# Sums of squares in column tiles, state products ahead of the last third of the output products, and drained blocks ahead of the weights' low part, in a Mamba-2 mixer on one core

## What is computed

```
proj = xn @ in_proj_w.T                       # gate 8192, hs 8192, B 1024, C 1024, dt 128
hBC  = silu(conv4(proj part) + conv_b)        # causal convolution of 4 taps
X    = hs * dt                                # 128 heads of 64 channels, chunks of 128 tokens
Y_diag = ((C B^T) * L) X                      # inside a chunk
states = (B * decay)^T X ; Y_off = C @ running states * exp(A_cs)
xg   = (Y_diag + Y_off + D*hs) * silu(gate)
xr   = xg * rsqrt(mean(xg*xg over a group of 1024 channels) + 1e-5)   # 8 groups
out  = (xr * norm_weight) @ out_proj_w.T      # 8192 -> 512
```

## Time and profile before

| | us |
|---|---|
| median of 3 runs | 1606.25 (1604.5 to 1606.3) |
| the profiled execution, its own time | 1604.1 |
| its span from the first to the last instruction | 1602.4 |
| PE busy in it | 1578.8 (99%) |
| DVE, ACT, POOL busy | 1423.1, 1370.4, 1279.1 |
| granted PE clock | 1.000 |

### The profile page before, as it was taken

One profiled execution on the slowest core, in us unless ns is written; L12 is line 12 of the kernel. 1 busy time (PEld: TensorE's weight loads), 2 busy tenths in 40 slices (PEclk: granted clock), 3 DMA queues, 4 the chain that ended last, 5 costly groups with the idle time before them and its releaser, 6 DMA issues. The chain is left out here.

```text
span 1602.4 us, 29224 instructions
## 1 busy us (share of the span) xinstructions
PE 1578.8 (99%) x9172; PEld 1296.0 (81%) x9172; DVE 1423.1 (89%) x2328; ACT 1370.4 (86%) x2620; POOL 1279.1 (80%) x1614
## 2 busy tenths in 40 slices
PE   9999999999999999999999999999999999999998
PEld 7877888888888888887778788888888888888886
DVE  7989899999999998999979888888888898888887
ACT  4688899999999898988846899989999999899895
POOL 5549998989898998989874487877777777778786
PEclk9999999999999999999999999999999999999999
DMA  5266767677767676676614666766766677667662
GB/s 175 93 186 205 227 188 218 201 209 214 195 218 206 201 224 199 206 206 198 196 40 145 204 208 200 225 202 202 227 189 218 207 204 222 199 205 227 190 218 89
DMA packets 231754, 311.83 MB, mean 195 GB/s; under 512 B 144176, under 2 KB 160560, under 8 KB 231344
## 3 DMA queue, kind: packets, MB, share of 16 engines
q1 hardware_dynamic: 231600, 309.97, 63.9%
HBM read 240.69 MB, written 36.70 MB: 173 GB/s over the span
## 5 line engine op out<-in xcount | busy, mean ns | idle before, releaser
L409 ACT ACTIVATE mt<-cs_row,cs_tok 128x128 f32<-128x128 f32 x1024 | 324.9, 391 | 0.0
L633 POOL TENSOR_TENSOR wl<-raw,wh 128x256 fp32r<-128x256 f32 x328 | 254.4, 807 | 59.3 <-ACT wh L381 59.3
L727 POOL COPY xt<-turned 128x512 uint16<-128x512 uint16 x248 | 206.3, 878 | 58.6 <-DMA turned<-tg 58.2
L718 POOL TENSOR_TENSOR mt<-mt,gt 128x256 f32<-128x256 f32 x128 | 117.8, 942 | 134.3 <-ACT mt L590 134.3
L743 POOL TENSOR_TENSOR sqa<-sqa,sq 128x256 f32<-128x256 f32 x222 | 221.6, 1018 | 0.8 <-ACT sq L563 0.8
L750 POOL TENSOR_TENSOR wol<-raw_o,woh 128x256 fp32r<-128x256 f32 x256 | 183.3, 737 | 39.0 <-ACT woh L530 38.9
L736 POOL TENSOR_TENSOR xl<-xg,xh 128x256 fp32r<-128x256 f32 x254 | 192.2, 778 | 5.1 <-ACT xh L543 5.1
L1093 DVE SCALAR_TENSOR_TENSOR cv<-bt,par_sb,cv 128x511 f32<-128x511 f32 (+2 forms) x192 | 143.8, 749 | 42.5 <-ACT cv L385 37.9
L1093 DVE SCALAR_TENSOR_TENSOR cv<-bh,par_sb,cv 128x511 f32<-128x511 f32 (+2 forms) x192 | 143.7, 748 | 30.8 <-ACT cv L385 25.8
L1323 DVE TENSOR_TENSOR mt<-mt,gt 128x1024 f32<-128x1024 f32 (+1 forms) x128 | 159.7, 1247 | 0.9 <-ACT mt L590 0.9
L381 ACT ACTIVATE wh<-raw 128x1024 fp32r<-128x1024 f32 (+1 forms) x146 | 151.9, 1040 | 0.8 <-DMA raw<-in_w_dtag 0.8
(11 more groups left out here) (217 smaller groups left out, 3819.2 us busy)
## 6 DMA issues: line engine op xcount, KB each, us to landing
raw<-in_w_step SPq DMA_DIRECT2D x128, 512.0 KB, 4.5
cs_row<-cs_rows SPq DMA_DIRECT2D x128, 512.0 KB, 7.0
low_parts<-wl SPq DMA_DIRECT2D x64, 512.0 KB, 5.8
raw_o<-in_w_out SPq DMA_DIRECT2D x128, 256.0 KB, 5.7
wl<-low_parts SPq DMA_DIRECT2D x64, 512.0 KB, 4.7
ec_row<-ec_rows SPq DMA_DIRECT2D x256, 96.0 KB, 5.7
raw<-in_w_bc SPq DMA_DIRECT2D x16, 512.0 KB, 3.5
acc<-in_x SPq DMA_DIRECT2D x8, 256.0 KB, 5.0
```

The source lines that it names most:

```text
L409: e = act.activation(mt[:, m % 2, h, chunk(j)], cs_row[:, m % 2, h, chunk(j)], ACT.Relu, bias=cs_tok[:, j, 2 * m + h:2 * m + h + 1], scale ...
L633: e = pool.tensor_tensor(wl[:, n % 2, cols], raw[:, n % 2, cols], wh[:, n % 2, cols].bitcast(F32), ALU.subtract)
L727: e = pool.tensor_copy(to[:, half], turned[:, NJ * half:NJ * (half + 1), :])
```

## The change

It does five things:

1. `sum_squares` makes the ones (128 by 32) the stationary operand and moves the squares, 128 columns for each of four column tiles of 32. The sums of 32 tokens lie along the free axis, copied to 32 rows of a tile. `mean_square` scales 128 by 128 values into rows and transposes them in blocks of 32 by 32, so that the four columns wanted stand at every 32nd place; both live in `part[:, 0]`, and two waits are added for that (`p_acc` of the group before, `p_lo`).
2. In steps 2 to 63 `output` issues two thirds, then the state products follow, then the last third, then the diagonal products.
3. The wait for `xt` is moved from the state products to the diagonal products (where the tokens were turned by DMA; steps 0 and 63 keep it).
4. In b = 1 `add_drained` adds all three blocks in one step, ahead of `wol`.
5. The dead branches for `TURN_FROM` go, with `pick` and its reduction.

```diff
-        ones = sb("ones", [P, 1])
+        ones = sb("ones", [P, SQ])
+        ms_rows, ms_cols = part[:, 0, P:2 * P], part[:, 0, 0:P]
+        ms = part[:, 0, 0:P:SQ]
...
+                    if b + 1 == NB and has(m - 2) and m > 2 and (m - 2) % PER_GROUP == 0:
+                        add_drained(b, (n - 2) // PER_GROUP - 1, range(ACT_BLOCKS))
                     if has(m - 1):
                         pool.wait_ge(a_woh, did(n - 1))
...
-                    if has(m - 2) and m > 2 and (m - 2) % PER_GROUP == 0:
+                    if b + 1 < NB and has(m - 2) and m > 2 and (m - 2) % PER_GROUP == 0:
                         add_drained(b, (n - 2) // PER_GROUP - 1, range(ACT_BLOCKS - 1))
-                    if has(m - 2) and m > 3 and (m - 3) % PER_GROUP == 0:
+                    if b + 1 < NB and has(m - 2) and m > 3 and (m - 3) % PER_GROUP == 0:
                         add_drained(b, (n - 3) // PER_GROUP - 1, (ACT_BLOCKS - 1,))
...
+                    early_state = has(m) and has(m - 2) and by_dma(b, m - 1)
+                    def sum_squares(dst, src, start=True, stop=True):
+                        of = src[:, :].rearrange("p (j a c) -> p a j c", j=NJ, c=SQ)
                         for a in range(P // SQ):
+                            mm = pe.matmul(dst[SQ * a:SQ * (a + 1), 0:P].rearrange("p (j c) -> p j c", j=NJ), ones[:, :],
+                                           of[:, a], start=start, stop=stop)
+                        return mm
-                        for j in range(NJ):
-                            mm = pe.matmul(dst[:, j:j + 1], sqa[:, chunk(j)], ones[:, 0:1],
-                                           start=True, stop=True)
...
                         if has(m - 2):
-                            output()
+                            output(range(2) if early_state else range(3))
...
                         pe.wait_ge(v_xd, did(n - 1))
-                        pe.wait_ge(v_x, did(n - 1))
+                        if not by_dma(b, m - 1):
+                            pe.wait_ge(v_x, did(n - 1))
...
                         mm.then_inc(t_st, 1)
+                        if early_state:
+                            output((2,))
                         yb = bank_y(b, m - 1)
+                        pe.wait_ge(v_x, did(n - 1))
                         pe.wait_ge(v_m, did(n - 1))
...
-                        for j in range(NJ):
-                            pe.matmul(bt[:, j:j + 1], sqa[:, chunk(j)], ones[:, 0:1], start=True, stop=False)
-                            mm = pe.matmul(bt[:, j:j + 1], sq[:, chunk(j)], ones[:, 0:1], start=False, stop=True)
-                        mm.then_inc(t_ss, 1)
+                        sum_squares(bt, sqa, stop=False)
+                        sum_squares(bt, sq, start=False).then_inc(t_ss, 1)
...
                 dve.wait_ge(t_ss, did(g))
-                dve.tensor_scalar(ms[:, :], src[:, 0:NJ], 1.0 / (INTER // GROUPS), 4 * EPS, ALU.mult, ALU.add).then_inc(v_ms, 1)
+                dve.wait_ge(p_acc, did(g - 1, ACT_BLOCKS))
+                dve.wait_ge(p_lo, g // GROUPS + 1)
+                dve.tensor_scalar(ms_rows, src[:, 0:P], 1.0 / (INTER // GROUPS), 4 * EPS, ALU.mult, ALU.add).then_inc(v_some, 1)
+                dve.wait_ge(v_some, did(g))
+                dve.transpose(ms_cols, ms_rows).then_inc(v_ms, 1)
```

More of the change, by code:

```diff
@@ L58 @@
 SQ = 32
-TURN_FROM = 0
 def mixer_kernel(nc, x, w_step, w_bc, w_dtag, w_out, par, headpar, w_ffn, w_b, b_ffn, b_gate, out):
@@ L208, in by_dma @@
         def by_dma(b, m):
-            return b >= TURN_FROM and 1 <= m < STEPS - 1
+            return 1 <= m < STEPS - 1
         def turn(b, m):
-            return (b - TURN_FROM) * (STEPS - 2) + m - 1
+            return b * (STEPS - 2) + m - 1
         def turned_by_pe(b, m):
-            return b * STEPS + m if b < TURN_FROM else TURN_FROM * STEPS + 2 * (b - TURN_FROM) + (m > 0)
+            return 2 * b + (m > 0)
         def wait_turned(eng, b, m):
@@ L925, in _, with output @@
                     ends = has(m - 2) and (m - 2) % PER_GROUP == PER_GROUP - 1
[L927 to L932, removed]
-                        for a in range(P // SQ):
-                            mm = pe.matmul(bg[SQ * a:SQ * (a + 1), 0:NJ], pick[:, :], of[:, a, :], start=True, stop=True)
-                        mm.then_inc(t_ss, 1)
-                    def sum_squares(dst):
-                        pe.wait_ge(p_sqa, squares(b, m - 2))
-                        for j in range(NJ):
-                            mm = pe.matmul(dst[:, j:j + 1], sqa[:, chunk(j)], ones[:, 0:1],
-                                           start=True, stop=True)
-                        mm.then_inc(t_ss, 1)
-                    def output():
+                    early_state = has(m) and has(m - 2) and by_dma(b, m - 1)
+                    def sum_squares(dst, src, start=True, stop=True):
+                        of = src[:, :].rearrange("p (j a c) -> p a j c", j=NJ, c=SQ)
+                        for a in range(P // SQ):
+                            mm = pe.matmul(dst[SQ * a:SQ * (a + 1), 0:P].rearrange("p (j c) -> p j c", j=NJ), ones[:, :],
+                                           of[:, a], start=start, stop=stop)
+                        return mm
+                    def output(ks=range(3)):
                         first, very_last = (m - 2) % PER_GROUP == 0, n - 2 == NB * STEPS - 1
@@ L976, in output @@
                         else:
-                            for k, (a, c) in enumerate(parts):
+                            for k in ks:
+                                a, c = parts[k]
                                 wait_low(k)
@@ L983, in output @@
                                                    stop=False, skip_group_check=True)
-                        if not very_last:
+                        if not very_last and 2 in ks:
                             mm.then_inc(t_out, 1)
@@ L1036, in _ @@
                     if ends and m < STEPS:
[L1037 to L1041, removed]
+                        pe.wait_ge(v_h2, did(un))
+                        pe.wait_ge(p_sqa, squares(b, m - 2))
+                        sum_squares(mine, sqa).then_inc(t_ss, 1)
                     if m == STEPS and b + 1 < NB:
@@ L1371, in _ @@
                             mask_scores(b, GROUPS - 1)
-                        if ends and b < TURN_FROM:
-                            parts_of_squares(b, (n - 2) // PER_GROUP, m - 2)
-                        if b == 0 and m == 3:
-                            dve.tensor_reduce(pick[:, :], ident[:, :].rearrange("p (a c) -> p c a", c=SQ), AXX, ALU.add) \
-                                .then_inc(v_pick, 1)
                     if b + 1 < NB and STEPS - 12 <= m < STEPS - 6:
@@ L1389, in _ @@
                         next_state(b, m - 1, 2, other)
-                        if ends and b < TURN_FROM:
-                            mean_square((n - 2) // PER_GROUP, bg)
                         dve.wait_ge(t_d, did(n - 1))
@@ L1396, in _ @@
                                                  op0=ALU.mult, op1=ALU.add).then_inc(v_y1, 1)
-                        if ends and b >= TURN_FROM:
+                        if ends:
                             mean_square((n - 2) // PER_GROUP, mine)
```

20 lines of the change are left out of this document (5 added, 15 removed).

## The result

The changed kernel takes **1580.55 us** (median of 5 runs, 1579.59 to 1581.58) against 1605.24 in the same five rounds (1604.5 to 1606.3): ratio 0.9845 [0.9831 to 0.9859], 24.7 us less. The profiled execution has a span of 1578.9 us where that of before had 1602.4, at full granted clock. The forecast was 1582: 24 us off a median of 1606.25, which was that of the first three of these runs.

The account below looks back on a forecast made before the run. PE was taken as the bound, busy 1578.8 of 1602.4 us, with hidden waits for `xt`. Terms 21.0, 1.9, 1.0, 0.6 and 0.2 made 24.7; less 1, 24 us off 1606.25 gave 1582, range 1575 to 1595.

Parts of the forecast that it names:

- The loop through `xt`: Ordinary step: projection, ACT, DVE taps, `xd`, `xt`, state products, diagonal; PE's wait for `xt` costs 0.19 us in b=0, 0.12 in b=1.
- PE's new step 10.73 + 0.02 = 10.75: Ordinary step: PE's own 10.73 us plus 0.02 for state products followed by the last third.
- the two changes of kind: PE's new borders: state products to last third 0.02 us; last third to diagonal, net 0 against the old border's 0.09.
- a sign of being right: Expected in the new trace: the diagonal starts 0.91 to 1.0 us after the last third.
- (b): Rival: the new changes of matmul kind cost about 0.1 us a step more, 12 us in all: 1594; chance 0.09.
- (c): Rival: weights cannot be loaded ahead at the last third, both borders cost 0.19 us: 1626, slower; chance 0.06.
- At 434.4 at the earliest, and `xt` is done at 433.67: Moved wait at the diagonal in b=0: `xt` is ready before the diagonal can start, 0.7 us to spare, costing nothing.
- `xl`: PE's last third starts later, giving `xl` 0.67 us more; most of the 4.0 us of waits goes.
- rival a: State products wait for `xd` instead of `xt`, half of the ordinary gain goes, 5 to 7 us: 1588; chance 0.15.
- Rival (e): No effect: another loop of the same length stands behind `xt`, products with S waiting for DVE: 1605; chance 0.03.
- Sums of squares: At a group's end: column tiles take PE's sums from 1.02 us, saving 0.4 to 0.5 us per group.
- of the 0.45 only 0.2 is passed on: Group's end in b=0: DVE's longer `mean_square` lets `yo` start at 459.25 instead of 459.43, despite PE's saving.

## Why the prediction was right

By the steps of the prediction:

- **The loop through `xt`: right, sizes too.** It put the two delays at 0.11 and 0.08, and both went when the wait alone moved. With the wait kept and the loop made longer, the step grew by 0.63 in b=0 and 0.70 in b=1.
- **PE's new step 10.73 + 0.02 = 10.75:** measured 10.75 with the wait alone and 10.78 with the reorder, so the reorder costs 0.03. State products to last third takes 0.59 and last third to diagonal 1.10, together 1.69; the prediction had 0.67 + 0.91 = 1.58 and 0.11 for the two changes of kind, to the hundredth. Each of the two is right by itself, too: four matmuls of 512 columns behind fp32 records take 1.01 at any place (432.04 to 433.05), so 0.59 + 1.01 = 1.60 is 0.02 over 1.58, and 1.10 - 1.01 = 0.09 is left for the change into column tiles, the price of the old border. The 1.10 is outside the 0.91 to 1.0 that the prediction gave as a sign of being right, because that sign left out the 0.10 which the first border brings. From the last matmul of 512 columns to the diagonal it is 0.33, under the 0.35 named for rivals (b) and (c), and both fall. The rule of the Trainium skill, "TensorEngine Tiling (Array Packing)", Key Properties, that a change of tiling mode drains the array, agrees: there is one such change per step into the diagonal before and after, at 0.09 both times.
- **"At 434.4 at the earliest, and `xt` is done at 433.67":** 0.83 to spare, measured.
- **`xl`: right.** Ten waits have become one, and the kernels with and without the reorder tie that to it. It is worth 2.5 us at the end, 3.5 without the other parts.
- **`xd` in `xt`'s place (the 1 us taken off, and rival a):** it happens, but not in ordinary steps, where 0.28 us lie between `xd` and the state products. The trace has them within 0.06 of the end of `xd` in 14 steps, 13 of them in b=0: five of its first, the seven after a group's end (place 2, 11.02 against 10.78) and one more near its end. Before, there was none. Place 2 costs 7 x 0.24 = 1.7 us, and the first steps were as long before. So the margin was judged rightly where it was read, in an ordinary step, and not looked at behind a group's end, where `xd` being late costs some 0.24. Rival (e), that the products with S wait for DVE, holds in a small way at the same place: one step in eight of each sequence loses 0.2 to it, before as well in b=1.
- **Sums of squares: the mis-sized term.** "0.4 to 0.5 us less PE work per group" is 0.56; the eight records run four at a time. The 0.22 for four tiles at a time, with the 0.15 for the change, was near: 0.37 against the 0.36 measured. The Trainium skill, "TensorEngine Tiling (Array Packing)", Theoretical Speedup, gives up to four times for four tiles; here it is 2.6 (0.92 to 0.36), the change of mode included. DVE's part was well sized, 0.56 from the start of the scaling to `yo` against 0.6. What failed is "of the 0.45 only 0.2 is passed on": with the tiles alone place 1 is 0.56 shorter in both sequences, and no later place takes it back. In b=0 the prediction let `mean_square` start at the old 458.66, but that start was itself set by the late sums: it came 0.80 after the start of the y product (457.86), and comes 453.70 - 453.04 = 0.66 after it now. With the tiles alone `yo` so came 0.36 sooner in place of 0.2, and DVE's chain behind it got another 0.33 shorter, which the prediction did not have. In b=1 "ACT is in the way" was the wrong reading of a missing idle mark. ACT's `xh` starts 2.86 after the products with S before (1256.08 and 1253.22) and 2.89 after them now (1239.22 and 1236.33): It had idled 1.22 in front of `xh`, waiting for `xg`, and idles 0.67 now, so it hangs on those products and moves with them.
- **The POOL edit, "0 on PE":** alone it gives 3.2 us, by the very stall that the prediction had counted under `xl`. In the sum this did no harm; as a price of the edit it was wrong.
- **The group:** 1.6 and 1.4 us were forecast; the medians give 88.9 - 87.0 = 1.9 and 88.4 - 86.9 = 1.5. The first groups gave less than the 1.9 + 1.0 forecast: b=0 nothing (seven intervals of 78.4 us before and after), b=1 0.5. Steps 4 to 6 of b=0 take 11.45 to 11.47, set by POOL's bias additions, which the prediction had not looked at; moving them shows it. Steps 5 and 6 had taken that before, and step 4 rose to it from 11.10, so what step 2 gained was lost again.
- **Tail:** sums to output products is 0.97 now (1571.92 - 1570.95) against 1.78, but the stretch from the last products with S to the end of the span shrank by 0.5 (13.53 to 13.06), near the 0.6 forecast.

So the mechanism of the loop was right, and that the sum before its rounding, 24.7, is the measured figure is luck: an undersized sums-of-squares term (some 3 us too little over the fourteen intervals between ends) and oversized first groups (2.4 too much) nearly balance. Of the 1.4 us between 1582 and 1580.55, 1.0 is the start from 1606.25, where the median of all five runs was 1605.24.

## What to carry to other kernels

Measure steps from start to start: a stall shorter than the tail of a matmul record is counted as busy, and up to 0.19 us of it in every step was 12.8 us here, of which PE's list of waits before had marked 2.9 for `xt`. Put each wait at the first instruction that reads the data; a wait one group of matmuls too early can close a loop through three engines, and a reorder without moving the wait can make that loop longer (here by 79 us). Price two edits that remove the same stall together, since their gains don't add. A reorder that costs 0.03 a step where nothing is late can be limited to the steps where an operand is; that this pays was not shown, since the engine that is behind was met at its next product instead.

## What the runs showed of the hardware that was not expected

- Eight fp32 matmuls of one column with a 128x128 stationary operand start 0.112 us apart, as those of 128 columns do: 0.92 us for sums that move four columns' worth of data. With `ones` as a stationary operand of 32 columns in four column tiles, the records of four tiles start 0.007 apart, the two sets of four 0.114 apart, and the products with S 0.202 after the last record.
- The state products in fp32 take 0.67 to the next fp32 products but only 0.59 when matmuls of 512 columns follow; the four of 512 columns then take 1.01 in place of 0.91, most of it between the first and the second (0.314 in place of 0.227). The two together are 0.02 dearer. The change into the two column tiles of the diagonal costs 0.09, from fp32 in the full array (0.76 against 0.67) as from 512 columns (1.10 against 1.01).
- From the end of `xt` to the state products it took 0.15 us where they waited for it, from the end of `xd` 0.05 or 0.06. What makes the difference was not tried.
- DVE's block transposition of 128x128 fp32 took 0.31 us and its scaling out of PSUM 0.28, both close to the prediction's 0.25.
- The same kernel had medians of 1580.55 and 1582.01 us on two chips, beside 1605.24 and 1605.59. Differences of 1.5 us between kernels of different jobs say nothing here.
